# First layer's heads: the fills for the row maxima as eight 64-by-32 matmuls, and the two fills of a unit set apart

## The chip, the cores and the metric

The kernel runs on one core of a Trainium2 chip. The metric is the device time of one execution in microseconds; the kernel before took 2050.77 us (median of three runs, 2050.46 to 2055.49).

## The reference

Four layers follow each other; each is `x = x + attention(norm(x)) * silu(feed_forward(norm(x)))` on 2048 tokens of 128 features. The change is in the first layer's attention, which has 16 heads of 8 features and no causal mask:

```
scores = jnp.einsum('bhtd,bhsd->bhts', q, k) * scale      # 16 heads, 2048 x 2048, over 8 features
attn = jax.nn.softmax(scores, axis=-1)
out = jnp.einsum('bhts,bhsd->bhtd', attn, v)
```

The other three layers, their feed-forwards and the projections stay as they are.

## The kernel before

`attention_heads` (from L478) does all heads of a layer; the first layer calls it with `causal` false and the fourth with `causal` true. Queries and keys are kept as stacks: each is split into three bf16 parts, and the rows of a stack hold the products of parts that are wanted, 72 rows in all, in `qs` and `ks`. For the first layer a copy of the first 64 rows of a head's stacks lies in partitions 64 to 127 of `qd` and `kd`.

A head's softmax needs each row's maximum first. So the work on a head comes in two passes.

**The pass for the maxima.** `runs` lists a head's 32 items: for each of 16 blocks of 128 queries, two items of two banks (512 keys each). An item is one *fill* on TensorE (`fill`, L670) and one *take* on VectorE (`take`, the reduction at L808). A fill is two matmuls (L686): the first contracts rows 0 to 63 (`qs`, `ks`), the second rows 64 to 127 (`qd`, `kd`), each gives 128 queries by 512 keys, and each writes its own bank of `pM`. Only 64 of the 72 rows go into the maxima. `pM` has four banks (`FILLED`), so two fills can be open: a fill waits until the take of the fill before the last is over (`taken`), and a take waits for its fill (`filled`).

**The main pass.** It has 16 *units* a head, each 128 keys by 2048 queries. A unit is four *chunks*: `score_chunk` computes a score of 128 keys by 512 queries (75 rows: 72 of the stacks and three that hold the maxima). Its line calls `by_columns` (L661), which splits the 128 columns of the fixed operand into four groups of 32, one matmul each (L664). ScalarE exponentiates a chunk (L785) into `probs`. Then `sum_unit` (L726) multiplies the unit's four blocks of probabilities by the values, four matmuls of 128 rows by 32 columns in f32, which accumulate in `pO`. `pS` has three banks (`RING`), so chunks run three ahead of the exponentials.

**The order on TensorE** is written out in `one_head`. For each unit it issues the sum of this unit, then the next four chunks, and between these the unit's share of fills for the next head. `ahead(u)` gives each unit two items, ten items ahead of the main pass (`LEAD`); before the loop all 32 items of the first head and ten of the second are filled, the 32 with steps of the first feed-forward between them (L890 to L896, 128 rows by 128 columns). Where in a unit the fills stand is set by `behind`: for each item the number of chunks ahead of it. Before, both are 2 in the first layer, so both fills stand next to each other in the middle. In unit 12 `turn` (L696) transposes the next head's maxima, a 128-by-128 matmul; it waits for `split`, the last of VectorE's chain of five small operations (L823 to L833) behind the 32nd take.

**The order on VectorE** (`one_head` of its block) is two takes a unit; ahead of the last unit's takes it copies the finished sums of the head from `pO` to `ot` (L842), which TensorE's first sum of the next head waits for. SyncE loads the stacks of the head after the next, each transfer released by a count of chunks scored (L592). Of the last head no fills are left: the last 21 units of the layer (11 to 15 of head 14 and all 16 of head 15) have none.

Of the kernel before, what the change touches and what calls it, by code (L numbers as in the profile page):

```python
# [17 lines left out]
P = 128  # L18
NT = T // P
BLK = 512  # L20
# [457 lines left out]
def attention_heads(nc, K, layer, causal, scatter=None, spread=()):  # L478
# [6 lines left out]
    ROUND = 3  # L485
# [18 lines left out]
    def ahead(u):  # L504

        return [(1, j) if j < ITEMS else (2, j - ITEMS) for j in range(upto[u] + LEAD, upto[u + 1] + LEAD)]

    with Stage(nc, f"heads{layer}") as S:
        qs = [S.sb(f"qs{i}", [P, T], BF16) for i in range(ROUND)]
        ks = [S.sb(f"ks{i}", [P, T], BF16) for i in range(ROUND)]  # L510

        qd = None if causal else [S.sb(f"qd{i}", [P, T], BF16) for i in range(ROUND)]
        kd = None if causal else [S.sb(f"kd{i}", [P, T], BF16) for i in range(ROUND)]
# [11 lines left out]
        pM = S.ps("pM", [P, FILLED, BLK])  # L525
# [23 lines left out]
        def exists(p, c):  # L549

            return not isinstance(p, int) or ROUND * p + c < HEADS
# [107 lines left out]
        def _(pe):  # L659
            def by_columns(out, still, moving, start, stop):  # L660

                for g in range(P // VW):
                    cols = slice(g * VW, (g + 1) * VW)
                    mm = pe.matmul(out[cols, :], still[:, cols], moving, start=start, stop=stop)  # L664
                return mm

            def bank_of(c, j, k):
                return (BLOCKS * c + before[j] + k) % FILLED

            def fill(p, c, j):  # L670

                n = BLOCKS * (ROUND * p + c) + before[j + 1]
                i, blocks, _ = runs[j]
                if j == 0:
                    pe.wait_ge(stacked[c % ROUND], 16 * LOADS * (p + c // ROUND + 1))
                if not isinstance(n, int) or n > FILLED:
                    pe.wait_ge(taken, n - FILLED)
                if causal:
                    (b, w), = blocks
                    bank = pM[:, bank_of(c, j, 0), :]  # L680
                    mm = by_columns(bank[:, 0:w], qs[c % ROUND][0:STK, i * P:(i + 1) * P],
                                    ks[c % ROUND][0:STK, b * BLK:b * BLK + w], True, True)
                else:
                    for k, (b, w) in enumerate(blocks):
                        rows = slice(k * HALF, (k + 1) * HALF)
                        mm = pe.matmul(pM[:, bank_of(c, j, k), 0:w], (qs, qd)[k][c % ROUND][rows, i * P:(i + 1) * P],  # L686
                                       (ks, kd)[k][c % ROUND][rows, b * BLK:b * BLK + w], start=True, stop=True)
                mm.then_inc(filled, 1)

            def turn(p, c, event):  # L690

                e, slot = event
                if not isinstance(e, int) or e >= RING:
                    pe.wait_ge(exped, e - RING + 1)
                pe.wait_ge(split, ROUND * p + c + 1)
                pe.transpose(pS[:, slot, :].bitcast(BF16)[:, 0:P], max_parts[:, :, :].rearrange("p a t -> p (a t)"),  # L696
                             K.ident_b[:, :]).then_inc(scored, 1)

            def score_chunk(p, c, n):

                h = ROUND * p + c
                _, _, u, _, c0, c1, _ = chunks[n]
                e = EVENTS * h + place(p, c, n) + 1
                slot = (EVENTS * c + place(p, c, n) + 1) % RING
                if n == 0:
                    pe.wait_ge(rows_in, 16 * PARTS * (h + 1))
                if not isinstance(e, int) or e >= RING:
                    pe.wait_ge(exped, e - RING + 1)
                diag = causal and c0 == u * P
                mm = by_columns(pS[:, slot, 0:c1 - c0], ks[c % ROUND][0:STK + PARTS, u * P:(u + 1) * P],  # L710
                                qs[c % ROUND][0:STK + PARTS, c0:c1], True, not diag)
                if diag:
                    mm = by_columns(pS[:, slot, 0:P], K.ident_b[:, :], K.neg_below[:, :], False, True)
                mm.then_inc(scored, 1)

            def sum_unit(p, c, u):

                h = ROUND * p + c
                if u == 0:
                    pe.wait_ge(v_in, h + 1)  # L720
                    pe.wait_ge(ot_kept, h + 1)
                pe.wait_ge(exped, EVENTS * h + place(p, c, first_chunk[u + 1] - 1) + 2)
                for k, (t, b, c0, c1, second) in enumerate(units[u]):
                    group = [n for n, ch in enumerate(chunks) if (ch[1], ch[6]) == (k, second)]
                    o = c0 - b * BLK
                    mm = pe.matmul(pO[k * 32:k * 32 + VW, int(second), o:BLK], vh[c][:, t, :],  # L726
                                   probs[u % 2][:, k * BLK + o:(k + 1) * BLK], start=first_chunk[u] + k == group[0],
                                   stop=first_chunk[u] + k == group[-1])
                mm.then_inc(used, 1)

            def one_head(p, c):
                for u in range(NU):
                    sum_unit(p, c, u)
                    new = [(c + n // NC, n % NC) for n in range(first_chunk[u + 1] + RING, first_chunk[u + 2] + RING)]
                    new = [(d, n) for d, n in new if exists(p, d)]
                    todo = [(c + d, j) for d, j in ahead(u) if exists(p, c + d)]
                    behind = [-(-(i + 1) * len(new) // (len(todo) + 1)) if causal else len(new) // 2
                              for i in range(len(todo))]
                    for k in range(len(new) + 1):
                        for (d, j), at in zip(todo, behind):  # L740
                            if at == k:
                                fill(p, d, j)
                        if k < len(new):
                            d, n = new[k]
                            if d == c and n == TURN_AT and exists(p, c + 1):
                                turn(p, c + 1, (EVENTS * (ROUND * p + c) + TURN_AT + 1, (EVENTS * c + TURN_AT + 1) % RING))
                            score_chunk(p, d, n)
# [5 lines left out]
            for j in range(ITEMS):  # L753
                fill(0, 0, j)
                if feed and j % 2 == 1 and AT_ONCE + j // 2 < feed.STEPS:
                    feed.pe_step(pe, AT_ONCE + j // 2)
            if feed:
                feed.pe_done(pe)
            for j in range(SLACK):
                fill(0, 1, j)  # L760
# [3 lines left out]
            for n in range(first_chunk[1] + RING):  # L764
                score_chunk(0, 0, n)
            every_head(one_head)

        @block.scalar
# [1734 lines left out]
```

## Time and profile before

| | us |
|---|---|
| median of three runs (lowest, highest) | 2050.77 (2050.46, 2055.49) |
| the profiled execution | 2040.68 |
| its span | 2038.9 |
| 13 heads of the first layer, from 149.23 to 688.25 | 539.02 |
| one of them, mean | 41.46 |

The busy shares over the span are TensorE 84%, VectorE 72%, ScalarE 56%, GpSimd 14%. Busy time is where at least one instruction of an engine ran. "PE" is TensorE's matmuls, "PEld" its weight loads, which overlap them; "DVE" is VectorE, "ACT" ScalarE, "POOL" GpSimd. In the timeline, instructions of one line that follow closely are merged: "x8" with 0.62 us are eight that began at the time shown and ended 0.62 us later in all. A matmul's duration holds its way through the array, so neighbours overlap, and the distance from start to start is what one costs. A number with "*" is the shape: 75*32 is 75 rows by 32 columns of the array, 75x512 the moved operand.

### The profile page before, as it was taken

What the parts mean: (1) busy time and instruction counts of PE and PEld (TensorE: products, weight loads), DVE (VectorE), ACT (ScalarE), POOL (GpSimd) and SP (SyncE); (2) the same over time, 40 slices, a digit from 0 to 9 for tenths busy, and PEclk for the clock granted to TensorE, in tenths of its full rate; (3) what the DMA queues carried; (4) which work ended last, traced back from release to release, by engine and by line L of the source; (5) the groups of instructions that cost most, each with busy time, mean ns of one, the idle gap of its engine ahead of it and who ended that gap; (6) DMA issues with size and microseconds to landing.
All of it is one profiled execution on the core that took longest, in us unless ns stands there. A gap on an engine that the chain in (4) does not pass through costs nothing. (4 is left out here: it accounts for less than half of the span.)

```text
span 2038.9 us, 44089 instructions
## 1 busy us (share of the span) xinstructions
PE 1716.2 (84%) x17561; PEld 819.0 (40%) x17561; DVE 1462.0 (72%) x2798; ACT 1139.9 (56%) x2246; POOL 284.5 (14%) x394
## 2 busy tenths in 40 slices
PE   4699999999999986799987787783579999999967
PEld 2222222232232224344435445672324444555546
DVE  5889999999999925855566036435878888899725
ACT  3278888888888881322212333342216676777744
POOL 1000000000000000000003244323012222211123
PEclk8799999999999997999987889787759999999988
DMA  4011112211111021052323387641410111111032
GB/s 137 32 55 62 49 49 73 65 54 48 66 50 36 3 47 65 3 127 84 92 84 127 104 289 248 206 112 39 176 53 26 36 34 35 30 29 28 13 86 79
DMA packets 78037, 154.52 MB, mean 76 GB/s; under 512 B 18684, under 2 KB 35964, under 8 KB 74136
## 3 DMA queue, kind: packets, MB, share of 16 engines
q1 hardware_dynamic: 63152, 121.57, 19.1%
q0 software_dynamic: 14384, 29.29, 4.6%
q8 instruction: 139, 2.28, 0.5%
q10 hardware_dynamic: 296, 0.85, 0.1%
q14 instruction: 66, 0.54, 0.1%
HBM read 102.23 MB, written 48.89 MB: 74 GB/s over the span
## 5 line engine op out<-in xcount | busy, mean ns | idle before, releaser
L785 ACT ACTIVATE heads_probs<-heads_pS 128x512 f32<-128x512 f32 (+3 forms) x1664 | 857.9, 573 | 233.9 <-PE heads_pS L664 211.1
L808 DVE TENSOR_REDUCE heads_run_max<-heads_pM 128x1 f32<-128x1024 f32 x512 | 598.9, 1219 | 50.2 <-PE heads_pM L686 47.8
L664 PE MATMUL heads_pS<-heads_qs,heads_ks 75*32 75x512 bf16 (+3 forms) x6656 | 598.3, 372 | 17.4 <-ACT heads_probs L785 14.6
L726 PE MATMUL heads_pO<-heads_probs,heads_vh 128*32 128x512 f32 (+2 forms) x3328 | 437.6, 571 | 3.2 <-ACT heads_probs L785 1.4
L664 PEld LDWEIGHTS heads_pS<-heads_qs,heads_ks 75*32 75x32 bf16 x6656 | 185.9, 95 | 319.1 <-ACT heads_probs L785 170.1
L664 PE MATMUL heads_pM<-heads_ks,heads_qs 72*32 72x512 bf16 (+3 forms) x2560 | 274.9, 370 | 14.1 <-DMA heads_qs<-k_parts_dram 8.4
L819 DVE TENSOR_REDUCE heads_run_max<-heads_pM 128x1 f32<-128x512 f32 x384 | 247.7, 685 | 30.3 <-PE heads_pM L664 27.7
L686 PE MATMUL heads_pM<-heads_ks,heads_qs 64*128 64x512 bf16 x512 | 182.8, 394 | 44.2 <-DVE heads_run_max L808 29.7
L572 POOL DMA_DIRECT2D k_head_out_dram<-heads_ot x120 | 62.6, 529 | 880.8 <-DVE heads_ot L842 644.6
L686 PE MATMUL heads_pM<-heads_kd,heads_qd 64*128 64x512 bf16 x512 | 182.9, 394 | 0.0
L1507 DVE TENSOR_REDUCE second_row_max<-second_banks 128x1 f32<-128x2048 f32 (+15 forms) x16 | 20.7, 1291 | 168.1 <-PE second_banks L1465 118.1
L664 PEld LDWEIGHTS heads_pM<-heads_ks,heads_qs 72*32 72x32 bf16 x2560 | 93.8, 97 | 115.8 <-DVE heads_run_max L819 47.0
L816 DVE CUSTOM_DVE_ANT_0 heads_masked_out<-heads_pM,heads_mask_end 128x128 bf16<-128x128 f32 (+3 forms) x256 | 122.0, 486 | 23.3 <-PE heads_pM L664 14.9
L726 PEld LDWEIGHTS heads_pO<-heads_probs,heads_vh 128*32 128x32 f32 x3328 | 104.4, 111 | 68.1 <-issue 10.0
L686 PEld LDWEIGHTS heads_pM<-heads_ks,heads_qs 64*128 64x128 bf16 x512 | 47.3, 93 | 206.8 <-DVE heads_run_max L808 104.1
L1298 ACT ACTIVATE top_act_gate<-top_pG 128x512 f32<-128x512 f32 x68 | 40.7, 598 | 133.8 <-PE top_pU L1273 133.8
L1325 DVE TENSOR_TENSOR top_hidden<-top_act_gate,top_pU 128x512 f32<-128x512 f32 x68 | 46.8, 688 | 79.4 <-ACT top_act_gate L1298 79.4
L664 PE MATMUL heads_pS<-k_neg_below,k_ident_b 128*32 128x128 bf16 x1024 | 85.8, 222 | 0.0
L2003 POOL DMA_INDIRECT k_x_slots_dram<-k_xn,k_place_i x32 | 31.3, 978 | 376.8 <-DVE k_place_i L1875 367.4
L1272 PE MATMUL top_pG<-k_xnT,k_gate 128*128 128x512 f32 x128 | 66.3, 600 | 4.3 <-PEq L65 4.3
L1278 PE MATMUL top_pY<-top_hidden,k_down 128*128 128x512 f32 x128 | 66.1, 598 | 3.0 <-DVE top_hidden L1331 2.9
L1753 PE MATMUL second_banks<-second_w,second_hT 128*96 128x128 f32 x384 | 54.8, 290 | 15.2 <-ACT second_hT L1804 11.6
(375 smaller groups left out, 2016.0 us busy)
## 6 DMA issues: line engine op xcount, KB each, us to landing
top_weights<-k_comb_dram SPq DMA_DIRECT2D x128, 128.0 KB, 3.0
second_w<-in_L_W_dram SPq DMA_DIRECT2D x12, 1024.0 KB, 9.3
k_hid_slots_dram<-k_zeros SPq DMA_DIRECT2D x8, 1152.0 KB, 4.7
k_h_slots_dram<-second_work SPq DMA_DIRECT2D x48, 192.0 KB
second_work<-k_hid_slots_dram SPq DMA_DIRECT2D x48, 192.0 KB
k_parts_dram<-proj_part SPq DMA_DIRECT2D x12, 512.0 KB, 4.0
heads_qs<-k_parts_dram SPq DMA_DIRECT2D x64, 96.0 KB
heads_ks<-k_parts_dram SPq DMA_DIRECT2D x60, 96.0 KB
```

The costliest lines, as they stand in the source:

```text
L572: queue.dma_start(K.head_out[h, :, b * BLK:(b + 1) * BLK], ot[c][b * 32:b * 32 + HD + 1, 0, :])\
L664: mm = pe.matmul(out[cols, :], still[:, cols], moving, start=start, stop=stop)
L686: mm = pe.matmul(pM[:, bank_of(c, j, k), 0:w], (qs, qd)[k][c % ROUND][rows, i * P:(i + 1) * P], (ks, kd)[k][c % ROUND][rows, b * BLK:b * B ...
L726: mm = pe.matmul(pO[k * 32:k * 32 + VW, int(second), o:BLK], vh[c][:, t, :], probs[u % 2][:, k * BLK + o:(k + 1) * BLK], start=first_chunk ...
L785: act.activation(probs[u % 2][:, k * BLK + c0 - b * BLK:(k + 1) * BLK], pS[:, slot, 0:c1 - c0], ACT.Exp)\
L808: dve.reduce_max(run_max[:, i, blocks[0][0] // 2:blocks[0][0] // 2 + 1], both.rearrange("p k c -> p (k c)"), AX.X).then_inc(taken, 2)
L816: dve.tensor_tensor_reduce(masked_out[:, i % TPB, 0:w], pM[:, bank, 0:w], mask_end[:, BLK - w:BLK], 1.0, LOWEST, ALU.add, ALU.max, run_max ...
L819: dve.reduce_max(run_max[:, i, b:b + 1], pM[:, bank, 0:w], AX.X).then_inc(taken, 1)
L1272: pe.matmul(pG[:, n % 2, :], gw, x, start=True, stop=True)
L1278: pe.matmul(pY[:, :], w, hidden[:, n % 2, :], start=(n == 0), stop=(n == L1_J)).then_inc(downed, 1)
L1325: mix = dve.tensor_tensor(hidden[:, n % 2, :], act_gate[:, n % 2, :], pU[:, n % 2, :], ALU.mult)
L1753: pe.matmul(pY[0:R, n % 2, 0:D], hT[:, n % 2, f, :], w[:, e, f * D:(f + 1) * D], start=(f == 0), stop=False)
```

## The change

`fill` calls `by_columns` for the first layer too. Each of its two matmuls becomes four, 64 rows by 32 columns, over the same 512 keys and into the same bank; the semaphore goes up with the last of the eight. `behind` becomes 1 for a unit's first fill and 3 for its second, so that the order is sum, chunk, fill, chunk, chunk, fill, chunk. The fourth layer's fills and places are unchanged.

```diff
                 else:
                     for k, (b, w) in enumerate(blocks):
                         rows = slice(k * HALF, (k + 1) * HALF)
-                        mm = pe.matmul(pM[:, bank_of(c, j, k), 0:w], (qs, qd)[k][c % ROUND][rows, i * P:(i + 1) * P],
-                                       (ks, kd)[k][c % ROUND][rows, b * BLK:b * BLK + w], start=True, stop=True)
+                        mm = by_columns(pM[:, bank_of(c, j, k), 0:w], (qs, qd)[k][c % ROUND][rows, i * P:(i + 1) * P],
+                                        (ks, kd)[k][c % ROUND][rows, b * BLK:b * BLK + w], True, True)
                 mm.then_inc(filled, 1)
...
-                    behind = [-(-(i + 1) * len(new) // (len(todo) + 1)) if causal else len(new) // 2
+                    behind = [-(-(i + 1) * len(new) // (len(todo) + 1)) if causal else 1 + 2 * i
                               for i in range(len(todo))]
```

## Rows read from the trace of the kernel before

**Rows 1.** The page, part 1: busy time of each engine over the span.
```profile
PE 1716.2 (84%) x17561; PEld 819.0 (40%) x17561; DVE 1462.0 (72%) x2798; ACT 1139.9 (56%) x2246; POOL 284.5 (14%) x394
```

**Rows 2.** Timeline of VectorE: start us, us; the first copy of a head's sums.
```profile
149.23 0.68 DVE L842 COPY heads_ot<-heads_pO 128x512 f32<-128x512 f32 x1
```

**Rows 3.** Busy us by stretch (x): PE, PEld, DVE, ACT, POOL; granted clock, DMA share, GB/s.
```profile
149.23:688.25 539.02, 516.33 (x5839) 160.18 (x5839) 505.06 (x495) 455.59 (x846) 30.82 (x65) 1.00 0.16 53
```

**Rows 4.** Waits from 149.23 to 605.41: total us, times, longest us.
```profile
PEld heads_pM L686 <- DVE heads_run_max L808: 54.7, 111, 0.8
DVE heads_run_max L808 <- PE heads_pM L686: 25.1, 66, 0.5
```

**Rows 5.** Timeline of TensorE's matmuls over two units, start us, us.
```profile
403.27 0.39 PE L686 MATMUL heads_pM<-heads_ks,heads_qs 64*128 64x512 bf16 x1
403.28 0.39 PE L686 MATMUL heads_pM<-heads_kd,heads_qd 64*128 64x512 bf16 x1
403.50 0.38 PE L686 MATMUL heads_pM<-heads_ks,heads_qs 64*128 64x512 bf16 x1
...
403.81 0.62 PE L664 MATMUL heads_pS<-heads_qs,heads_ks 75*32 75x512 bf16 x8
404.25 1.03 PE L726 MATMUL heads_pO<-heads_probs,heads_vh 128*32 128x512 f32 x8
405.11 0.60 PE L664 MATMUL heads_pS<-heads_qs,heads_ks 75*32 75x512 bf16 x8
405.65 0.39 PE L686 MATMUL heads_pM<-heads_ks,heads_qs 64*128 64x512 bf16 x1
...
406.19 0.39 PE L686 MATMUL heads_pM<-heads_ks,heads_qs 64*128 64x512 bf16 x1
...
406.51 0.61 PE L664 MATMUL heads_pS<-heads_qs,heads_ks 75*32 75x512 bf16 x8
...
408.88 0.40 PE L664 MATMUL heads_pS<-heads_qs,heads_ks 75*32 75x512 bf16 x4
```

**Rows 6.** Timeline of VectorE over the same two units.
```profile
403.77 4.73 DVE L808 TENSOR_REDUCE heads_run_max<-heads_pM 128x1 f32<-128x1024 f32 x4 [0.46 <-PE heads_pM L686]
408.85 1.23 DVE L808 TENSOR_REDUCE heads_run_max<-heads_pM 128x1 f32<-128x1024 f32 x1 [0.34 <-PE heads_pM L686]
```

**Rows 7.** Timeline of the weight loads of two chunks.
```profile
403.81 0.12 PEld L664 LDWEIGHTS heads_pS<-heads_qs,heads_ks 75*32 75x32 bf16 x8 [0.34 <-ACT heads_probs L785]
```

**Rows 8.** Timeline of TensorE: the first feed-forward's matmuls, two fills, and back.
```profile
62.13 0.39 PE L895 MATMUL heads_pS<-k_squares,heads_probs 128*128 128x128 f32 x2
62.35 0.39 PE L896 MATMUL heads_pS<-k_rows_of,k_ident 128*128 128x128 f32 x2
62.67 0.39 PE L686 MATMUL heads_pM<-heads_ks,heads_qs 64*128 64x512 bf16 x1
...
62.90 0.38 PE L686 MATMUL heads_pM<-heads_ks,heads_qs 64*128 64x512 bf16 x1
...
63.21 0.38 PE L895 MATMUL heads_pS<-k_squares,heads_probs 128*128 128x128 f32 x1
```

**Rows 9.** Timeline of TensorE: a sum, the transpose of the maxima, chunks.
```profile
180.74 1.03 PE L726 MATMUL heads_pO<-heads_probs,heads_vh 128*32 128x512 f32 x8
181.71 0.23 PE L696 MATMUL heads_pS<-k_ident_b,heads_max_parts 128*128 128x128 bf16 x1
181.87 0.61 PE L664 MATMUL heads_pS<-heads_qs,heads_ks 75*32 75x512 bf16 x8
```

**Rows 10.** Timeline of VectorE: ten takes with no wait between them.
```profile
94.64 11.40 DVE L808 TENSOR_REDUCE heads_run_max<-heads_pM 128x1 f32<-128x1024 f32 x10
```

**Rows 11.** Timeline of VectorE: first operation of the chain, and the take behind the chain.
```profile
179.96 0.22 DVE L823 TENSOR_REDUCE heads_neg_max<-heads_run_max 128x16 f32<-128x64 f32 x1
...
180.93 1.22 DVE L808 TENSOR_REDUCE heads_run_max<-heads_pM 128x1 f32<-128x1024 f32 x1
```

**Rows 12.** The page, part 5: all takes of the first layer.
```profile
L808 DVE TENSOR_REDUCE heads_run_max<-heads_pM 128x1 f32<-128x1024 f32 x512 | 598.9, 1219 | 50.2 <-PE heads_pM L686 47.8
```

## The prediction

> **What bounds the kernel now.** I began with the page's busy shares and slices [rows 1]: TensorE is busy 84% of the span, the highest share, but that share doesn't tell which stage can give time back. So I cut out the stage that the change touches. VectorE's copies of the summed heads mark it. The first stands at 149.23 [rows 2], and from there to the fourteenth, at 688.25, are 13 heads in 539.02 us, 41.46 us a head. In that stretch TensorE is busy 516.33 us, VectorE 505.06, ScalarE 455.59, and the granted clock is 1.00 [rows 3]. TensorE and VectorE are both near their limit, so I asked who waits for whom: before a fill's weight loads TensorE waits 54.7 us for VectorE's maxima, and VectorE 25.1 us for fills [rows 4]. Each holds up the other in turns.
>
> The timeline shows how [rows 5]. Two kinds of unit alternate. From 406.51 to 408.88, 2.37 us, TensorE never waits. From 403.81 to 406.51, 2.70 us, its second fill waits until 406.19 for a bank. The mean is 2.54 us. VectorE takes the two units' four fills in 4.73 us and then stands idle 0.34 us, because both fills of the next unit come late and together [rows 6].
>
> Inside a unit I read distances from start to start [rows 5]. A sum takes 0.86 us (404.25 to 405.11), a chunk behind a chunk 0.21 to 0.22 (two in 0.44), and a fill behind a fill 0.23 (403.27 to 403.50). But from the chunk before a fill to the fill it is 0.54 − 0.22 = 0.32 us (405.11 to 405.65), and from the fill back to a chunk 0.31 in a pair and 0.32 alone (406.19 to 406.51). So each change of shape costs 0.10 us, and a unit has two of them. The interval behind a change is 0.23 rather than 0.21. Check: 0.86 + 0.21 + 0.32 + 0.23 + 0.31 + 0.23 + 0.21 = 2.37.
>
> **The change, part by part.**
>
> *Four column groups.* A fill's two matmuls, 64 rows by 128 columns, become eight, 64 by 32. The arithmetic and the moved rows are the same. Two row halves already run at once, 0.01 us apart (403.27 and 403.28), and so do four column groups: the four matmuls of the chunk at 408.88 take 0.40 us together, where a single one takes 0.39 [rows 5]. I take all eight to run at once. The last of four starts within 0.01 us of the first, some 0.003 us a start, so the last of eight starts some 0.02 us later than the last of two; the engine has to come to the end of it before it changes shape. Bounds: nothing, and 0.04. I take 0.02, from that row. The six added weight loads per fill are covered as in a chunk, whose eight loads stand in 0.12 us beside its matmuls [rows 7]; that is priced at nothing, and uncovered it would be at most those 0.12 us.
>
> *Does the change of shape go away?* A fill would share its column width with chunks and sums, but not its rows: they have 75 and 128, it has 64. The trace has no 64 by 32 matmul. It has a change of rows alone: from the gate's 128-by-128 matmuls to a fill at 62.67 [rows 8]. Two of these stand in 0.22 us (62.13 to 62.35), so the last began at 62.46, and 0.21 passes to the fill where 0.11 is the pace; back, 62.90 to 63.21, is 0.31. The same 0.10 each way. It has a change of columns alone as well: a sum, 128 by 32, to the 128-by-128 transpose takes 0.97 us instead of 0.86 (180.74 to 181.71), and 0.16 back [rows 9]. Rows alone, columns alone and both together cost the same. So I keep 0.10 us per change; the other end is nothing.
>
> This is also where the Trainium skill speaks against the change: TensorEngine Tiling (Array Packing), section Tiling Modes, lists 64×32 apart from 128×32 and says that a change of mode, not of tile, drains the engine. By that rule the 0.10 us stays, and the rows above agree with it.
>
> *The two fills stand apart,* before the second and the fourth of a unit's four chunks. Each is now alone between chunks, so a unit has four changes in place of two. Its distances: sum 0.86, into a fill 0.32, out 0.32, chunk 0.23, into a fill 0.32, out 0.32, chunk 0.23: 2.60 us. With 0.02 for each fill's later last start, 2.64. In exchange the waits go. VectorE needs 1.13 us a take (ten in 11.40 us, of which the last has 1.22: 10.18 for nine) [rows 10], so 2.26 a unit, against 2.64; a bank is free 1.7 us after its fill starts if VectorE is free (0.50 from 403.27 to 403.77, and 1.22) and some 2.0 if the other take comes first, and the next fill into it comes 2.6 us later. The 2.70 us unit disappears, and so does the 2.37 us one. What is late next is the fill: VectorE will stand idle some 0.38 us a unit, and TensorE never.
>
> *Per head:* 16 × 2.64 = 42.24, and 0.27 for the transpose (0.97 + 0.16 for 0.86) [rows 9]: 42.5 us. VectorE's chain of five (0.97 us, 179.96 to 180.93) [rows 11] and its copy (0.68 [rows 2], of which some 0.08 overlaps the take behind it, as takes do) delay takes once each, and fit into the slack: 0.38 a unit and a bank's 0.6. Against 41.46 that is +1.0 us. Without the later starts it is 41.6 + 0.27 = 41.87, +0.4; with 0.04 a fill it is 43.2, +1.7.
>
> *How many units?* Of 512 takes [rows 12], 32 serve the first head and 10 the second before the loop; the other 470 are fills in 235 units, 14.7 heads' worth. The 42 ahead are at VectorE's pace (the last ten in one run of 11.40 us [rows 10]), so their later starts are hidden; uncovered, 42 × 0.02 is 0.8 us. No DMA is added or moved. The stacks' loads are released by chunk counts, and the second fill moves past one chunk: nothing. The transpose's wait for the chain lies a unit and more behind the last fill of its head, so its cover stays. The last 21 units have no fills and stay as they are.
>
> Sum: 14.7 × 1.0 = **+15 us** (bounds +6 and +25). The profiled execution took 2040.68 us, its span 2038.9; it becomes 2056. The median of the runs is 10.1 us above the profiled one, and the same addition gives 2066, so I forecast **2065**.
>
> The skill's other rule here, TensorE: Matmul & The Clock Gate, Part 3 (packing small matmuls), adds about 4 ns per tile to the duration of one. By it eight tiles cost 0.03 us over one, close to my 0.02.
>
> **Rivals.** About 0.3%, 6 us, is what a measurement of this kernel can tell from no change.
>
> *Nothing is drained between equal column widths.* The place is the chunk-to-fill distance: it falls to 0.22. TensorE then needs 0.86 + 6 × 0.215 = 2.15 us a unit and VectorE becomes the bound: 32 × 1.13 + 0.97 + 0.60 = 37.7 us a head, above TensorE's 34.7 and ScalarE's 35.0 (455.59 / 13 [rows 3]). That is −3.7 × 14.7 = −55 us: 1996. It decides from the point where the 0.10 falls below some 0.085: today's head leaves (41.46 − 0.27) / 16 = 2.57 us a unit, 0.07 less than my 2.64, and four changes share that. For it speaks that the column groups could hand over one by one; against it the 62.67 rows. Chance 0.20. If a row-only change is cheaper here without being free (0.03 to 0.08), the head lies between 38 and 41.2: about 2025. Chance 0.06.
>
> *The two row halves take turns inside a column group.* Each fill then costs 0.22 more, 32 × 0.22 = 7 us a head, 103 us on top of the 15: 2169. The pair at 403.27 and 403.28 speaks against it. Chance 0.05. The same without changes of shape gives 0.86 + 8 × 0.215 = 2.58 a unit and about 2051 to 2055. Chance 0.03.
>
> *The change doesn't do what it says:* every unit with fills has two of them and four chunks, so positions 1 and 3 always exist. No chance of its own.
>
> **How the numbers follow.** My own case has 0.66. Its range is 2056 to 2073, and an eighth of its chance lies below +6 us. The range must take in the free case to leave out no more than 2 in 10: 1996 to 2073. Faster: 0.20 + 0.05 = 0.25. Same: 0.08 + 0.03 + 0.01 = 0.12. Slower: 0.58 + 0.05 = 0.63.
>
> **What would show it.** In the changed profile, units of one length, 2.60 to 2.64 us, with no alternation; each fill 0.32 us behind its chunk; TensorE's waits for maxima near nothing and VectorE's for fills up from 25 us to some 90 (235 × 0.38); head copies 42.5 us apart; 20,633 matmuls. A chunk-to-fill distance of 0.22 and VectorE busy throughout would prove me wrong downward; fills 0.5 us long upward.

## The result and the profile after

The changed kernel takes 2066.14 us (median of four, 2063.99 to 2069.71) against 2050.61 for the kernel before: a ratio of 1.008, with a 95% interval of 1.006 to 1.01. It is 15.5 us slower, where 15 were forecast.

The answer to [rows 3] and [rows 1] of the changed kernel: first the page's busy times, then the busy time by stretch, over the same 13 heads (PE, PEld, DVE, ACT, POOL, then the granted clock).

```profile
PE 1759.8 (85%) x20633; PEld 809.5 (39%) x20633; DVE 1463.1 (71%) x2798; ACT 1138.2 (55%) x2246; POOL 284.2 (14%) x394
...
150.06:701.34 551.28, 551.28 (x8341) 149.43 (x8333) 506.17 (x495) 455.24 (x846) 30.83 (x65) 1.00 0.16 52
```

The 13 heads take 551.28 us instead of 539.02, 42.41 a head instead of 41.46. TensorE now has a matmul in flight in all of them: 551.28 us busy of 551.28. VectorE and ScalarE do the same work in the same time as before (506.17 and 455.24). So the added time is TensorE's own, at an unchanged clock.

Where in a unit it lies, the timeline of TensorE shows, with the same columns as [rows 5]:

```profile
403.99 0.39 PE L664 MATMUL heads_pS<-heads_qs,heads_ks 75*32 75x512 bf16 x4
404.31 0.40 PE L664 MATMUL heads_pM<-heads_ks,heads_qs 64*32 64x512 bf16 x4
404.32 0.40 PE L664 MATMUL heads_pM<-heads_kd,heads_qd 64*32 64x512 bf16 x4
404.65 0.61 PE L664 MATMUL heads_pS<-heads_qs,heads_ks 75*32 75x512 bf16 x8
405.19 0.40 PE L664 MATMUL heads_pM<-heads_ks,heads_qs 64*32 64x512 bf16 x4
...
405.53 0.40 PE L664 MATMUL heads_pS<-heads_qs,heads_ks 75*32 75x512 bf16 x4
405.76 1.03 PE L727 MATMUL heads_pO<-heads_probs,heads_vh 128*32 128x512 f32 x8
406.62 0.39 PE L664 MATMUL heads_pS<-heads_qs,heads_ks 75*32 75x512 bf16 x4
```

From the chunk to the fill it is 0.32 us (403.99 to 404.31), from the fill back 0.34 (404.31 to 404.65), and the same again at 405.19 and 405.53. The unit is 2.63 us long (403.99 to 406.62), and the next ones are as long; the alternation of 2.37 and 2.70 is gone. The two row halves start 0.01 us apart, in all four column groups: all eight matmuls run at once.

The waits (total us, times, longest) from 150.06 to 616.53, in answer to [rows 4]:

```profile
DVE heads_run_max L809 <- PE heads_pM L664: 35.7, 131, 0.6
PEld heads_pM L664 <- DVE heads_run_max L809: 17.5, 35, 0.6
```

TensorE's wait for takes has fallen from 54.7 to 17.5 us, and those 17.5 stand beside running matmuls. VectorE's wait for fills has risen from 25.1 to 35.7.

The last head's copy begins at 776.35 in the profiled execution, and began at 762.17 before: the stage holds 14.2 us of the difference. Of these, 12.3 lie in the 13 heads, 1.1 in the two heads behind them and 0.8 ahead of the first copy. The two profiled executions differ by more, 2064.07 against 2040.68. Part of that is in the third layer, which the change doesn't touch. There the stretch with the most traffic took 378.54 us after and 368.92 before, with VectorE's and ScalarE's work alike, and no run shows why; the rows are the changed kernel's and the kernel before's:

```profile
1082.29:1460.83 378.54, 254.64 (x1560) 188.29 (x1560) 165.12 (x481) 127.01 (x265) 126.34 (x128) 0.80 0.50 160
```

```profile
1066.04:1434.96 368.92, 250.50 (x1561) 186.17 (x1561) 164.97 (x481) 127.16 (x265) 126.52 (x128) 0.82 0.50 164
```

The medians, 15.5 us apart, leave little beyond the 14.2.

### The profile page after: what moved, and what is told of

It reads as the page before. It is cut to its first block and busy times, and to the rows that moved or that the text cites. A ratio compares the mean times of both kernels' runs of the same rounds, so it can differ in the third digit from the quotient of the medians.

```text
span 2062.3 us, 50233 instructions
## 1 busy us (share of the span) xinstructions
PE 1759.8 (85%) x20633; PEld 809.5 (39%) x20633; DVE 1463.1 (71%) x2798; ACT 1138.2 (55%) x2246; POOL 284.2 (14%) x394
## 5 line engine op out<-in xcount | busy, mean ns | idle before, releaser
L664 PE MATMUL heads_pS<-heads_qs,heads_ks 75*32 75x512 bf16 (+3 forms) x6656 | 640.0, 373 | 17.9 <-ACT heads_probs L786 14.7
L664 PE MATMUL heads_pM<-heads_ks,heads_qs 64*32 64x512 bf16 (+4 forms) x4608 | 481.3, 381 | 33.6 <-DVE heads_run_max L809 16.8
L664 PEld LDWEIGHTS heads_pM<-heads_ks,heads_qs 72*32 72x32 bf16 (+1 forms) x4608 | 143.8, 93 | 398.7 <-issue 246.4
L664 PE MATMUL heads_pM<-heads_kd,heads_qd 64*32 64x512 bf16 x2048 | 208.2, 397 | 0.0
L1299 ACT ACTIVATE top_act_gate<-top_pG 128x512 f32<-128x512 f32 x68 | 40.6, 597 | 134.3 <-PE top_pU L1274 134.3
L1274 PE MATMUL top_pU<-k_xnT,k_up 128*128 128x512 f32 x128 | 66.3, 599 | 0.0
L843 DVE COPY heads_ot<-heads_pO 128x512 f32<-128x512 f32 x32 | 21.9, 684 | 60.8 <-PE heads_pO L727 60.8
```

The source lines that it names most:

```text
L1274: pe.matmul(pU[:, n % 2, :], uw, x, start=True, stop=True).then_inc(opened, 1)
```

## The experiments

The theory: every change of rows or of columns costs TensorE 0.10 us, also between equal column widths; a fill's eight matmuls run at once; a later last start adds 0.02 us a fill. The first rival: the four times as many instructions cost, not the changes of shape. The second: changes between equal column widths are free. Seven kernels tell them apart; head lengths are 13 heads' time over 13, from copy to copy, and a unit's length is read from sum to sum.

### The column groups alone

```diff
-                        mm = pe.matmul(pM[:, bank_of(c, j, k), 0:w], (qs, qd)[k][c % ROUND][rows, i * P:(i + 1) * P],
-                                       (ks, kd)[k][c % ROUND][rows, b * BLK:b * BLK + w], start=True, stop=True)
+                        mm = by_columns(pM[:, bank_of(c, j, k), 0:w], (qs, qd)[k][c % ROUND][rows, i * P:(i + 1) * P],
+                                        (ks, kd)[k][c % ROUND][rows, b * BLK:b * BLK + w], True, True)
```

> The column groups alone: eight 64-by-32 matmuls a fill, but both fills in the middle of the unit, as before. Theory (every change of rows or columns costs 0.10 us, and the eight run at once): two changes a unit as before, and the 0.02 us of each fill's later last start; the two kinds of unit stay, near 2.4 and 2.7 us; a head goes from 41.46 to 41.6 or 41.8 us, and the time up by 2 to 5 us. Rival (the added instructions cost, 16 in place of 4 a fill): the whole +15 us is here, a head at 42.4. Second rival (equal column widths change for free, and it is the places that cost): a head near 40, 20 us faster than before.

2056.53 us against 2051.05, a ratio of 1.0029 (1.0015 to 1.0042): 5.5 us slower. TensorE's timeline over two units:

```profile
411.88 1.03 PE L726 MATMUL heads_pO<-heads_probs,heads_vh 128*32 128x512 f32 x8
...
414.27 1.03 PE L726 MATMUL heads_pO<-heads_probs,heads_vh 128*32 128x512 f32 x8
...
415.67 0.40 PE L664 MATMUL heads_pM<-heads_ks,heads_qs 64*32 64x512 bf16 x4
...
416.23 0.40 PE L664 MATMUL heads_pM<-heads_ks,heads_qs 64*32 64x512 bf16 x4 [0.16 <-DVE heads_run_max L808]
...
417.01 1.03 PE L726 MATMUL heads_pO<-heads_probs,heads_vh 128*32 128x512 f32 x8
```

The second fill still waits for a take (at 416.23, 0.56 us behind the first where a pair without a wait stands 0.23 apart), and the two kinds of unit are still there: sum to sum 2.39 us (411.88 to 414.27) and 2.74 (414.27 to 417.01), where before has 2.37 and 2.70. A head is 41.89 us (544.60 / 13). The column groups take nothing away, and cost 0.43 us a head, a little more than I expected (0.15 to 0.35). In the trace the unit without a wait is 0.02 us longer than before and the one with it 0.04. In the second kind the two fills stand apart, and a later last start counts twice: for the take that the second fill waits for, and for the chunk behind it. That makes three in two units, or 24 a head, which at 0.018 us each (see the next experiment) gives 0.43; no run isolates this. Both rivals fall in their full form, since one wanted 42.4 and the other 40.

### The places alone

```diff
-                    behind = [-(-(i + 1) * len(new) // (len(todo) + 1)) if causal else len(new) // 2
+                    behind = [-(-(i + 1) * len(new) // (len(todo) + 1)) if causal else 1 + 2 * i
```

> The places alone: fills of two 64-by-128 matmuls as before, the first ahead of a unit's second chunk, the second ahead of the fourth. Theory: four changes of shape a unit, 0.86 + 4 x 0.32 + 2 x 0.23 = 2.60 us, all units alike, TensorE never waits for a take; a head at 41.9 us, +6 us over before, so that this is the larger part of the changed kernel's +15. Rival (the added instructions cost): no more than before, or faster, since the waits for takes are gone: a head at 40 to 41.5.

2054.62 us, a ratio of 1.0023 (1.0008 to 1.0038). By stretch, 13 heads:

```profile
149.16:692.82 543.66, 543.66 (x5839) 141.98 (x5837) 505.95 (x495) 455.25 (x846) 30.82 (x65) 1.00 0.16 53
```

TensorE's timeline of one unit, from its sum to the next:

```profile
403.92 1.03 PE L726 MATMUL heads_pO<-heads_probs,heads_vh 128*32 128x512 f32 x8
...
405.97 0.39 PE L686 MATMUL heads_pM<-heads_ks,heads_qs 64*128 64x512 bf16 x1
...
406.29 0.40 PE L664 MATMUL heads_pS<-heads_qs,heads_ks 75*32 75x512 bf16 x4
406.51 1.03 PE L726 MATMUL heads_pO<-heads_probs,heads_vh 128*32 128x512 f32 x8
```

41.82 us a head where 41.9 was expected, all units 2.60 us but the transpose's, which is 2.87, and TensorE busy throughout. This is 0.36 us a head, some 5 us over 14.7 heads (the medians are 3.6 apart), with not one instruction added. The four changes of shape cost more than the waits that they replace. So what is added to a head has two parts: places 0.36 us a head and column groups 0.43, and together 0.95, 0.16 more than the sum. Where TensorE never waits, the later last start counts in every fill: 42.41 − 41.82 = 0.59 us over 32 fills is 0.018 us each. The single matmuls in the traces agree. In the changed kernel the eight of a fill start at 404.306 to 404.329 and the chunk at 404.646; before, the two of a fill start at 406.187 and 406.190 and the chunk at 406.507. From the last start to the chunk it is 0.317 us in both, and the last start lies 0.020 us later behind the first.

### All 72 rows in place of 64

The next two kernels have the changed kernel's places and its count of instructions. The first takes all rows of the stacks, so that the maxima are over 72 rows:

```diff
-                        mm = pe.matmul(pM[:, bank_of(c, j, k), 0:w], (qs, qd)[k][c % ROUND][rows, i * P:(i + 1) * P],
-                                       (ks, kd)[k][c % ROUND][rows, b * BLK:b * BLK + w], start=True, stop=True)
+                        mm = by_columns(pM[:, bank_of(c, j, k), 0:w], qs[c % ROUND][0:STK, i * P:(i + 1) * P],
+                                        ks[c % ROUND][0:STK, b * BLK:b * BLK + w], True, True)
```

> Fills with all 72 rows in four column groups, one bank after the other, the two fills apart as in the changed kernel; the count of instructions is that of the changed kernel, and the maxima are taken over all 72 rows instead of 64. Theory: 72 and 75 rows are one shape for the engine, so a fill follows a chunk at 0.22 us; the two banks take 0.43 us a fill; a unit is 0.86 + 8 x 0.216 = 2.59 us, a head 41.7, +4 us over before and some 11 faster than the changed kernel, although each fill streams twice as long. Rival (instructions, not changes of shape, cost): a head at 42.4 or above, since count and streaming only grow.

2062.37 us, a ratio of 1.0055 (1.0037 to 1.0073).

```profile
402.66 1.03 PE L726 MATMUL heads_pO<-heads_probs,heads_vh 128*32 128x512 f32 x8
403.52 0.39 PE L664 MATMUL heads_pS<-heads_qs,heads_ks 75*32 75x512 bf16 x4
403.74 0.60 PE L664 MATMUL heads_pM<-heads_ks,heads_qs 72*32 72x512 bf16 x8
404.17 0.60 PE L664 MATMUL heads_pS<-heads_qs,heads_ks 75*32 75x512 bf16 x8
404.61 0.61 PE L664 MATMUL heads_pM<-heads_ks,heads_qs 72*32 72x512 bf16 x8
...
405.26 1.03 PE L726 MATMUL heads_pO<-heads_probs,heads_vh 128*32 128x512 f32 x8
```

The mechanism came out as expected: chunk to fill is 0.22 us (403.52 to 403.74), and the fill's two banks take 0.43 (to 404.17). A unit is 2.60 us (402.66 to 405.26). The total did not: +11 us where I said +4. Two things were left out. A head is 42.05 us, because the transpose's unit is 3.04 us instead of some 2.87: its second fill waits for a take that VectorE's chain has put off. And the first head's copy stands at 154.40 instead of 149.23. Of these 5.2 us, 3.8 lie between the first take and the end of the 42nd (54.15 us, where before has 50.34): the fills ahead of the loop stream twice as long and are not all covered by VectorE. The rival fell on the unit length: as many instructions as in the changed kernel, and twice the streaming, in a shorter unit.

### 64 rows from one half

The same instructions again, in the same order and with the same banks, but with rows 0 to 63:

```diff
-                        mm = by_columns(pM[:, bank_of(c, j, k), 0:w], qs[c % ROUND][0:STK, i * P:(i + 1) * P],
-                                        ks[c % ROUND][0:STK, b * BLK:b * BLK + w], True, True)
+                        mm = by_columns(pM[:, bank_of(c, j, k), 0:w], qs[c % ROUND][0:HALF, i * P:(i + 1) * P],
+                                        ks[c % ROUND][0:HALF, b * BLK:b * BLK + w], True, True)
```

> As the kernel with whole rows, but each of a fill's eight matmuls takes rows 0 to 63 of the stacks instead of rows 0 to 71: count, order, banks and places of the instructions are the same, and only the number of rows differs. Theory (a change of rows alone drains the engine, and two matmuls on the same row half and column group take turns): a fill comes 0.31 to 0.32 us behind its chunk instead of 0.22, each unit pays four changes and both turns, near 3.05 us, a head 48.8 us, the time 105 to 110 us over before. Rival (only a change of columns costs, and in the changed kernel something else added the 0.10): a unit of 2.60 and a head of 42.05, as with whole rows. Second rival (changes cost, but the two banks' matmuls overlap even on one row half): near 2.63 us a unit, a head at 42.4.

This kernel and the two at the end were timed as a second group, on another chip, where the kernel before took 1960.64 us. The stretch of the third layer shown above took 301 us there (in the trace of the second alternating kernel) instead of 369. No kernel was profiled in both groups, but the first layer's units of one make have the same length in both: the two alternating kernels have units of 2.38 and 2.60 us. So I compare by ratio and by head. The ratio is 1.0682 (1.0635 to 1.073).

```profile
401.33 1.03 PE L726 MATMUL heads_pO<-heads_probs,heads_vh 128*32 128x512 f32 x8
402.20 0.39 PE L664 MATMUL heads_pS<-heads_qs,heads_ks 75*32 75x512 bf16 x4
402.52 0.61 PE L664 MATMUL heads_pM<-heads_ks,heads_qs 64*32 64x512 bf16 x8
403.06 0.62 PE L664 MATMUL heads_pS<-heads_qs,heads_ks 75*32 75x512 bf16 x8
403.60 0.61 PE L664 MATMUL heads_pM<-heads_ks,heads_qs 64*32 64x512 bf16 x8
404.14 0.40 PE L664 MATMUL heads_pS<-heads_qs,heads_ks 75*32 75x512 bf16 x4
404.37 1.03 PE L726 MATMUL heads_pO<-heads_probs,heads_vh 128*32 128x512 f32 x8
```

This is the sharpest pair of the study. With eight rows fewer and nothing else changed in the program, chunk to fill goes from 0.22 to 0.32 us (402.20 to 402.52) and fill to chunk from 0.43 to 0.54 (to 403.06). The unit goes from 2.60 to 3.04 us (401.33 to 404.37), and 0.44 over four changes is 0.11 each. A head is 48.86 us (635.24 / 13), where 48.8 was expected. So a change of rows alone costs what the theory says, and 72 and 75 rows count as one shape. The two banks' matmuls take turns when they use the same half: 0.54 us less the change of 0.11 is 0.43, against 0.34 less 0.11 for the changed kernel, whose two halves run side by side. The time rose by some 130 us rather than 105 to 110 (two runs, 15 us apart). The first copy stands at 170.61, 21.4 us later than in the profile of before. Some 4 of these are the fills ahead of the loop, as with whole rows. The other 17 are in the first head, more than double the 7.4 of each later one: its first four units are 5.60 us long. The granted clock is 0.50 there until 137 us and 1.00 from then on, with TensorE busy all the time (10.00 of the 10 us from 120 to 130); before, it is 1.00 from 110 us on. I had priced none of this, and no run shows why the clock rose so late.

### Alternating places

Back in the first group. If a change of shape costs 0.11 us and a wait 0.31 us every other unit, there is something in between: fills together in one unit, apart in the next. That is six changes in two units, where before has four and a wait, and the changed kernel eight.

```diff
-                    behind = [-(-(i + 1) * len(new) // (len(todo) + 1)) if causal else len(new) // 2
+                    behind = [-(-(i + 1) * len(new) // (len(todo) + 1)) if causal else (2 if u % 2 else 1 + 2 * i)
```

> Fills of two 64-by-128 matmuls as before; in even units they stand apart (places 1 and 3), in odd ones together (2 and 2). Theory: three groups of fills in two units, so six changes of shape where before has four and the changed kernel eight: TensorE needs 2.60 + 2.37 = 4.97 us for two units, less than the 5.07 that before takes with its wait of 0.31, and VectorE (4.53 for four takes) is served in time; a head at 40.5 us, 13 us faster than before. Rival (the fills' even spacing is what counts for VectorE): between before and the apart kernel, a head at 41.5 to 41.9.

2038.85 us against 2051.05: a ratio of 0.9944 (0.9925 to 0.9962), 12 us faster than before and, by the two ratios, some 28 faster than the changed kernel.

```profile
194.57 0.61 PE L664 MATMUL heads_pS<-heads_qs,heads_ks 75*32 75x512 bf16 x8
195.01 1.03 PE L726 MATMUL heads_pO<-heads_probs,heads_vh 128*32 128x512 f32 x8
195.88 0.39 PE L664 MATMUL heads_pS<-heads_qs,heads_ks 75*32 75x512 bf16 x4
196.20 0.39 PE L686 MATMUL heads_pM<-heads_ks,heads_qs 64*128 64x512 bf16 x1
...
197.07 0.39 PE L686 MATMUL heads_pM<-heads_ks,heads_qs 64*128 64x512 bf16 x1
...
197.61 1.03 PE L726 MATMUL heads_pO<-heads_probs,heads_vh 128*32 128x512 f32 x8
198.47 0.60 PE L664 MATMUL heads_pS<-heads_qs,heads_ks 75*32 75x512 bf16 x8
199.01 0.39 PE L686 MATMUL heads_pM<-heads_ks,heads_qs 64*128 64x512 bf16 x1
...
199.24 0.38 PE L686 MATMUL heads_pM<-heads_ks,heads_qs 64*128 64x512 bf16 x1
```

Sum to sum it is 2.60 us in the unit with the fills apart (195.01 to 197.61), and 2.38 with them together; at 199.24 the second fill follows the first in 0.23 us, with no wait. A head is 40.50 us (526.48 / 13), as expected. In the 13 heads TensorE is without a running matmul for 2.7 us, where before it was for 22.7: behind a unit whose fills stood apart, both banks are free in time for the pair. A part of the gain lies at the head's boundary: the transpose's unit is 3.13 us long instead of 3.35, and the one behind the copy 2.41 instead of 2.86.

### The alternation the other way round

```diff
-                    behind = [... if causal else (2 if u % 2 else 1 + 2 * i)
+                    behind = [... if causal else (1 + 2 * i if u % 2 else 2)
```

> The alternation the other way round: together in even units, apart in odd ones; the last unit of a head, in which VectorE also copies the sums, now has its fills apart, and the transpose's unit has them together. Theory (six changes of shape in two units is what counts): TensorE's own time is the same 4.97 us for two units, but the 16th unit and the copy now fall together, so a head between 40.5 and 41.4 us, faster than before by 1 to 14 us. Rival (the gain of the other order came from the head's boundary alone): at 41.5 us, no faster than before.

A ratio of 1.0008 (0.9995 to 1.0021), and 41.48 us a head: my range missed it by a little, and the rival's number came out. Both engines' timelines around the end of a head, at the unit that follows the copy:

```profile
189.51 0.68 DVE L842 COPY heads_ot<-heads_pO 128x512 f32<-128x512 f32 x1
...
190.11 4.60 DVE L808 TENSOR_REDUCE heads_run_max<-heads_pM 128x1 f32<-128x1024 f32 x4
...
191.72 0.39 PE L686 MATMUL heads_pM<-heads_ks,heads_qs 64*128 64x512 bf16 x1
...
192.51 0.39 PE L686 MATMUL heads_pM<-heads_ks,heads_qs 64*128 64x512 bf16 x1 [0.40 <-DVE heads_run_max L808]
```

TensorE's timeline of a unit with the transpose, in this kernel:

```profile
262.18 1.03 PE L726 MATMUL heads_pO<-heads_probs,heads_vh 128*32 128x512 f32 x8
...
264.88 0.39 PE L686 MATMUL heads_pM<-heads_ks,heads_qs 64*128 64x512 bf16 x1 [0.63 <-DVE heads_run_max L808]
...
265.64 1.03 PE L726 MATMUL heads_pO<-heads_probs,heads_vh 128*32 128x512 f32 x8
```

and in the first alternating kernel:

```profile
260.34 1.03 PE L726 MATMUL heads_pO<-heads_probs,heads_vh 128*32 128x512 f32 x8
...
263.47 1.03 PE L726 MATMUL heads_pO<-heads_probs,heads_vh 128*32 128x512 f32 x8
```

The ordinary units are 2.38 and 2.60 us here too. But the copy (0.60 us) and, four units ahead of it, the chain (0.97) put VectorE behind, and the unit that comes next has its fills together and needs two banks at once. So a grouped unit waits at both places in each head. Sum to sum, the one behind the copy is 2.96 us long, and the one with the transpose, behind the chain, 3.46: 0.58 and 1.08 over the 2.38 of a grouped unit. In the other order the unit with the transpose has its fills apart and is 3.13 us long, and the two grouped units that lag behind the chain and the copy are 2.48 and 2.41: 0.53, 0.10 and 0.03 over their kind. The difference, 1.00 us, is that between the two heads (0.98). So the rival was right on the number and half right on the cause: the ordinary units gain in both orders (2.49 in the mean, where before has 2.54), and at the head's boundary one order gives all of it back.

### Alternating places with the column groups

The places are those of the first alternating kernel, and the matmuls those of the column groups alone:

```diff
-                        mm = pe.matmul(pM[:, bank_of(c, j, k), 0:w], ...
+                        mm = by_columns(pM[:, bank_of(c, j, k), 0:w], ...
```

> The alternating places with the eight 64-by-32 matmuls of the changed kernel: what the column groups cost where TensorE hardly waits for takes. Theory: the later last start alone, 0.02 us for each of three groups of fills in two units, 0.5 us at most over the alternating kernel's head of 40.50: 40.8 to 41.0, the time 4 to 8 us over it and some 5 to 8 under before. Rival (the column groups cost as much as between before and columns alone only because a wait magnifies it): 40.5 to 40.6.

A ratio of 0.996 (0.9943 to 0.9977), and 40.83 us a head (530.80 / 13): 0.33 over the alternating kernel. The column groups are a plain cost here too, and smaller than with the old places (0.43) or where every fill stands alone (0.59). The rival, that only a wait makes them cost, wanted 40.5 to 40.6 and falls.

## Why the prediction was right

*The bound* was read rightly. In the 13 heads TensorE and VectorE held each other up, and once the fills stood apart TensorE was the bound alone, busy in all 551.28 us.

*The change of shape.* The step that decided the sign was to keep the 0.10 us between equal column widths, from the gate's matmuls at 62.67 [rows 8] although the change relies on the opposite. The pair of kernels with 72 and with 64 rows shows it directly, at 0.11. The Trainium skill's rule (TensorEngine Tiling (Array Packing), section Tiling Modes), that a change of mode drains the engine, agrees with that pair: 0.22 us from chunk to fill where mode and columns stay, 0.32 where only the rows change.

*The later last start*, 0.02 us a fill, measured 0.018. It was more than half of the forecast, and the choice to take it from the spread within a chunk was right: single starts show the last of a fill's matmuls 0.020 us later.

*Unit and head*: 2.64 forecast and 2.63 measured, 42.5 and 42.41, +1.0 and +0.95. The two kinds of unit, 2.37 and 2.70 us, were not the whole head before: the transpose's unit is 3.35 us long there (263.59 to 266.94) and the one behind the copy 2.86 (232.98 to 235.84), and in the changed kernel they are 2.91 and 2.63. The forecast missed nothing by it, since it set whole heads against each other. The stage grew by 14.2 us where 15 were forecast. That the medians are 15.5 apart, nearly the forecast, is in part luck: their interval goes from 12 to 21 us.

*The fills ahead of the loop* were priced at nothing, with 0.8 us if uncovered. They are covered, all but 0.1 us: from the first take to the end of the 42nd it was 50.34 us before (55.70 to 106.04) and is 50.48 in the changed kernel.

```profile
55.89 6.88 DVE L809 TENSOR_REDUCE heads_run_max<-heads_pM 128x1 f32<-128x1024 f32 x6 [8.63 <-PE heads_pM L664]
...
94.97 11.39 DVE L809 TENSOR_REDUCE heads_run_max<-heads_pM 128x1 f32<-128x1024 f32 x10
```

That the first copy came 0.83 us later, at 150.06, looks like the 0.8 but isn't: 0.48 of it arose behind the first head's first sum (107.56 before, 107.91 after), in its own units, and 0.19 ahead of the first take. Such a start differs between executions anyway: with the column groups alone, whose fills ahead are the same, the first take came at 57.68. The two experiments with longer fills show the limit of the cover, at 3.8 and 3.7 us.

*VectorE's wait for fills* was forecast too high. The 90 us are for 235 units, and the 35.7 measured are for 11 heads, 176 units, which makes the forecast 67. It also left out that the chain and the copy (1.57 us a head) fill part of the slack, 17 us, and took a take at 1.13 us, where VectorE's busy time in the 13 heads gives 1.17 (506.17 / 13 − 1.57, over 32), some 13 us. With these it would have been 37. This changed nothing in the sum.

*The rivals.* The free change fell with the 64-row pair and with the column groups alone. Row halves that take turns fell with the starts at 404.31 and 404.32; matmuls took turns only where both used the same rows. The price of that was forecast at 7 us a head, and is 6.45 where the experiment forces it (48.86 against 42.41).

## What to carry to other kernels

Count the changes of array shape per loop, rows and columns alike, and price each from a start-to-start distance in the trace: equal column widths do not save one where the rows differ as 64 and 75 do, while 72, 75 and 128 rows mixed freely, and here a fill set alone costs as much TensorE time as a fill that streams twice as long in its neighbours' shape. Splitting a matmul that has all 128 columns over column groups gained nothing here; it only started its last part later, for 0.33 to 0.59 us a head. Grouping saves changes and spacing saves waits, so try both within one period, and put the grouped unit where no other work of the consumer stands ahead of it.

## What was not expected

The order of the alternation decides all of its gain: 40.50 us a head in one and 41.48 in the other, with the same instructions and the same number of changes. And eight rows more made a matmul cheaper to place: 72 rows cost 0.22 us behind a chunk of 75, and 64 rows 0.32.
